# Self-attention's gate moved from the projected rows to the columns of its weight, and the order of every engine laid out anew

## What is computed

```python
attn_out = attn_out.transpose(0, 2, 1, 3).reshape(B, N, H)
attn_out = attn_out @ W_proj + b_proj
x = x + gate_a[:, None] * attn_out
q_c = _ln(x) @ W_qc + b_qc
```

## Time and profile before

| what | value |
|---|---|
| three runs, median (lowest to highest) | 2955.99 us (2954.45 to 2956.05) |
| the profiled execution, its own time | 2951.26 us |
| its span | 2949.5 us |
| mean granted clock of TensorE | 0.972 |
| PE busy | 2782.5 us, 94% |
| PE weight loads busy | 2278.2 us, 77% |
| VectorE busy | 1760.4 us, 60% |
| ScalarE busy | 1535.3 us, 52% |
| GpSimd busy | 700.2 us, 24% |

### The profile page before, as it was taken

The page is one execution under the profiler, slowest core; times in us unless marked ns, Lnnn a source line. Parts: engine busy times, 40 slices in busy tenths (PEclk is TensorE's granted clock), DMA queues, the critical chain, the costliest instruction groups (busy, mean ns, idle before and its releaser), DMA issues. The chain is left out here.

```text
span 2949.5 us, 61879 instructions
## 1 busy us (share of the span) xinstructions
PE 2782.5 (94%) x23508; PEld 2278.2 (77%) x23508; DVE 1760.4 (60%) x3583; ACT 1535.3 (52%) x2701; POOL 700.2 (24%) x760
## 2 busy tenths in 40 slices
PE   5999999994899999999999999999999999999997
PEld 4999999993577777777777777777777777777766
DVE  1344444434567777667667677666666666666642
ACT  2444444431356555555555565565565556555653
POOL 3344443331112222222222122122122121121211
PEclk7999999996699999999999999999999999999998
DMA  5222221003343443544554434544445435435421
GB/s 168 72 81 79 68 68 39 25 9 105 72 100 96 112 108 93 120 101 109 120 118 106 113 97 106 108 104 105 122 102 141 101 89 114 97 91 110 99 64 34
DMA packets 276951, 277.90 MB, mean 94 GB/s; under 512 B 90352, under 2 KB 206433, under 8 KB 276657
## 3 DMA queue, kind: packets, MB, share of 16 engines
q1 hardware_dynamic: 264752, 251.26, 35.8%
q10 hardware_dynamic: 11904, 22.68, 2.3%
HBM read 99.03 MB, written 29.56 MB: 44 GB/s over the span
## 5 line engine op out<-in xcount | busy, mean ns | idle before, releaser
L1544 ACT ACTIVATE p_f<-score 128x1024 f32<-128x1024 f32 (+1 forms) x576 | 560.6, 1019 | 340.2 <-PE obank L2165 157.9
L1821 DVE TENSOR_REDUCE m_a<-score 128x4 f32<-128x1024 f32 x384 | 457.6, 1217 | 51.9 <-PE score L2131 51.8
L2235 PE MATMUL gbank<-w,h_c 128*128 128x256 f32 x1536 | 401.4, 396 | 1.2 <-ACT h_c L1561 0.9
L2235 PEld LDWEIGHTS gbank<-w,h_c 128*128 128x128 f32 x1536 | 276.0, 192 | 48.3 <-ACT h_c L1561 1.1
L965 PE MATMUL m_ps<-m_comb,m_w 128*128 128x256 f32 x2304 | 300.5, 286 | 0.0
L965 PEld LDWEIGHTS m_ps<-m_comb,m_w 128*128 128x128 f32 x2304 | 284.8, 190 | 3.1 <-issue 1.7
L1425 POOL TENSOR_TENSOR res_a<-res_a,bias_a 128x512 f32<-128x512 f32 x48 | 64.6, 1346 | 666.9 <-DMA bias_a<-rows_L 666.9
L638 ACT ACTIVATE m_hf<-m_ps,tab 128x256 f32<-128x256 f32 x192 | 80.5, 470 | 253.3 <-PE m_ps L965 253.3
L580 POOL TENSOR_TENSOR m_hhl<-m_hf,m_hhl 128x512 fp32r<-128x512 f32 x96 | 125.2, 1304 | 328.8 <-DVE m_hhl L804 328.8
L2165 PE MATMUL obank<-p_f,v_s 128*20 128x256 f32 x3072 | 200.0, 391 | 0.0
L1433 POOL TENSOR_TENSOR c_rstd<-c_mv,eps 128x2 f32<-128x2 f32 x48 | 9.3, 194 | 774.6 <-DVE c_mv L1774 774.6
(11 more groups left out here) (234 smaller groups left out, 5561.2 us busy)
## 6 DMA issues: line engine op xcount, KB each, us to landing
k_cat<-k_hl SPq DMA_DIRECT2D x288, 128.0 KB, 3.6
q_cat<-q_hl SPq DMA_DIRECT2D x288, 128.0 KB, 4.2
qc_cat<-qc_hl SPq DMA_DIRECT2D x288, 128.0 KB, 3.2
split_L<-m_cut SPq DMA_DIRECT2D x24, 512.0 KB, 5.3
x_a<-x_after_L SPq DMA_DIRECT2D x48, 256.0 KB, 4.0
res_a<-x_after_L SPq DMA_DIRECT2D x48, 256.0 KB, 2.8
kc_cat<-kc_hl SPq DMA_DIRECT2D x288, 39.0 KB, 1.9
x_after_L<-y_c SPq DMA_DIRECT2D x32, 256.0 KB, 3.2
```

The costliest lines, as they stand in the source:

```text
L1544: e.activation(p_f[i % 4][0:n, :], score[i % 2].ap[0:n, :, :].rearrange("p h n -> p (h n)"), ACT.Exp, scale=SCALE).then_inc(ex.sem, 1)
L1821: e.tensor_reduce(m_a[:, :, i::NPAIR].rearrange("p t h -> p h t"), score[i % 2].ap[:, :, :].rearrange("p h (t k) -> p h t k", t=TT), AX.X, ...
L2235: mm = e.matmul(B_DOWN.ap[:, tt, :], h_c[:, k, tt * P:(tt + 1) * P], weights_of(d)["w2"][:, k, :], start=(k == 0), stop=(k == MC - 1))
```

## The change

Before, VectorE multiplied the projected rows by the gate and GpSimd added the residual. Now GpSimd multiplies the columns of w_o by the gate (`self_out_gated`, o_gated, one unit ahead), PE multiplies oT_a by o_gated, and VectorE adds x_b, which already holds x plus the bias, straight from the bank into x_b (`self_sum`). The tile res_a is gone: x is loaded into x_b. The loads, and the order of the calls on all five engines, are changed as well.

```diff
-                x_load(a, res_a, S["A_x"])
+                    e.wait_ge(*S["K_res"].at(a - 1))
+                    e.wait_ge(*S["K_xt"].at(a - 1))
+                x_load(a, x_b, S["A_x"])
...
-                    bias_added(res_a, res_a, bias_a[:, :], S["A_res"])
-
-            def self_sum(a):
-                if live(a):
-                    e.wait_ge(*S["T_y"].at(a))
-                    e.wait_ge(*S["A_res"].at(a))
-                    e.tensor_tensor(x_b[:, :, :], x_b[:, :, :], res_a[:, :, :], ALU.add).then_inc(S["T_xb"].sem, 1)
+                    bias_added(x_b, x_b, bias_a[:, :], S["A_res"])
+
+            def self_out_gated(a):
+
+                if not live(a):
+                    return
+                e.wait_ge(*S["A_gate"].at(a))
+                if a:
+                    e.wait_ge(*S["T_op"].at(a - 1))
+                if a % NB == 0:
+                    e.wait_ge(*W_in["o"].at(a // NB))
+                e.tensor_tensor(o_gated[:, :, :], W["o"][:, :, :], gate_a[:, :].unsqueeze(1).to_broadcast([P, CC, D]),
+                                ALU.mult).then_inc(S["T_og"].sem, 1)
...
-            def self_gated(a):
+            def self_sum(a):
                 if not live(a):
                     return
                 e.wait_ge(*S["T_op"].at(a))
-                e.wait_ge(*S["A_gate"].at(a))
-                if a:
-                    e.wait_ge(*S["K_res"].at(a - 1))
-                    e.wait_ge(*S["K_xt"].at(a - 1))
-                e.tensor_tensor(x_b[:, :, :], B_T.ap[:, :, :], gate_a[:, :].unsqueeze(1).to_broadcast([P, TT, D]),
-                                ALU.mult).then_inc(S["T_y"].sem, 1)
+                e.wait_ge(*S["A_res"].at(a))
+                e.tensor_tensor(x_b[:, :, :], B_T.ap[:, :, :], x_b[:, :, :], ALU.add).then_inc(S["T_xb"].sem, 1)
...
-                weights_in(a, "o")
-                turn(B_T, S["T_y"], a)
-                by_token(B_T, 0, oT_a, W["o"])
-                by_token(B_T, 1, oT_a, W["o"]).then_inc(S["T_op"].sem, 1)
+                e.wait_ge(*S["T_og"].at(a))
+                turn(B_T, S["T_xb"], a)
+                by_token(B_T, 0, oT_a, o_gated)
+                by_token(B_T, 1, oT_a, o_gated).then_inc(S["T_op"].sem, 1)
```

The order of GpSimd's calls, whole, since the prediction follows it:

```diff
-                context_rstd(n - 2)
+                context_rstd(a)
+                self_residual(a)
+                cross_rstd(a)
+                self_out_gated(n - 2)
+                mlp_sum(d)
+                mlp_residual(c)
+                self_rstd(n)
+                mlp_rstd(n - 4)
                 cross_residual(a)
-                self_residual(n - 2)
-                mlp_sum(n - 5)
-                self_rstd(n)
-                mlp_residual(n - 4)
-                self_sum(n - 2)
-                cross_rstd(n - 2)
-                mlp_rstd(n - 3)
```

More of the change, by code:

```diff
@@ L1134, in stats @@
             return sb(n + "_st", [P, TT, 6]), sb(n + "_mv", [P, TT, 2]), sb(n + "_rstd", [P, TT])
-        x_a, res_a = tile("x_a"), tile("res_a")
+        x_a = tile("x_a")
         xT_a, xT_b, xT_c = (sb(n, [P, 2, CC, NT], F32R) for n in ("xT_a", "xT_b", "xT_c"))
@@ L1141, in blocks @@
         bias_a, gate_a = sb("bias_a", [P, D]), sb("gate_a", [P, D])
+        o_gated = sb("o_gated", [P, CC, D])
         q_hl, k_hl = sb("q_hl", [P, 2, CC, NT], F32R), sb("k_hl", [P, 2, CC, NT], F32R)
@@ new lines, in _ @@
+                self_weights(n - 2, 7)
+                cross_max_high(n - 3)
+                next_queries_keys(q)
+                self_heads(n - 2, 0)
+                next_cross_queries(a)
+                next_rest(n)
+                next_up_high(c)
+                self_heads(n - 2, 1)
+                next_self_out(n - 2)
+                next_cross_out(b)
+                mlp_modulated(n - 4)
+                cross_weights(n - 3, 0)
+                cross_weights(n - 3, 1)
+                cross_weights(n - 3, 2)
@@ new lines, in _ @@
+                cross_weights(n - 3, 3)
+                cross_heads(n - 3, 0)
+                gelu_table(n - 4)
+                cross_heads(n - 3, 1)
+                next_values(n - 1)
+                mlp_act(n - 4, 0)
+                mlp_act(n - 4, 1)
+                mlp_act(n - 4, 2)
+                context_out(n - 2)
+                self_modulated(n)
+                self_max_high(n - 1)
+                cross_keys_high(n - 2)
+                next_up_low(n - 4)
+                cross_x_out(n - 2)
@@ L1762, in _ @@
+                keys_high(n)
+                mlp_act(n - 4, 3)
+                cross_queries_high(n - 2)
+                queries_high(n)
+                exp_table(n - 4)
+                self_weights(n - 1, 0)
+                self_weights(n - 1, 1)
+                self_weights(n - 1, 2)
+                self_weights(n - 1, 3)
+                self_weights(n - 1, 4)
+                self_weights(n - 1, 5)
         @block.vector
@@ L2404, in _ @@
                 self_plain(m, 2)
-                down(d, 6)
-                down(d, 7)
+                self_plain(m, 3)
+                mlp_turned(c)
+                values(m, 0)
                 cross_scores(b, 0)
-                self_plain(m, 3)
-                values(m, 0)
-                mlp_turned(c)
+                values(m, 1)
                 cross_scores(b, 1)
                 cross_scores(b, 2)
-                values(m, 1)
                 cross_values(b, 0)
+                up(c, 0)
@@ L2424, in _ @@
                 self_projected(a)
                 context_turned(a)
-                self_plain(m, 6)
-                self_plain(m, 7)
-                up(c, 2)
+                self_turned(q)
+                self_max_rows(m)
+                cross_keys_values(a)
+                keys(q)
+                cross_turned(a)
+                up(c, 3)
+                cross_queries(a)
+                cross_recips_spread(b)
+                queries(q)
+                self_scores(n - 2, 0)
+                self_scores(n - 2, 1)
@@ new lines, in _ @@
+                cross_projected(b)
+                down(n - 5, 0)
+                down(n - 5, 1)
+                down(n - 5, 2)
+                down(n - 5, 3)
+                down(n - 5, 4)
+                self_scores(n - 2, 2)
+                self_scores(n - 2, 3)
+                cross_plain(n - 3, 0, 0)
+                cross_plain(n - 3, 0, 1)
+                self_values(n - 2, 0)
+                cross_plain(n - 3, 1, 0)
+                self_scores(n - 2, 4)
+                cross_plain(n - 3, 1, 1)
@@ new lines, in _ @@
+                self_scores(n - 2, 5)
+                cross_plain(n - 3, 2, 0)
+                cross_plain(n - 3, 2, 1)
+                self_values(n - 2, 1)
+                cross_plain(n - 3, 3, 0)
+                self_scores(n - 2, 6)
+                self_scores(n - 2, 7)
+                cross_plain(n - 3, 3, 1)
+                down(n - 5, 5)
+                cross_max_rows(n - 3)
+                down(n - 5, 6)
+                self_plain(n - 1, 0)
+                self_plain(n - 1, 1)
```

183 lines of the change are left out of this document (55 added, 128 removed).

## The result

| | before | after |
|---|---|---|
| median, device us | 2955.3 (2954.45 to 2956.05, 4 runs) | 3037.3 (3032.17 to 3041.35, 4 runs) |
| profiled execution, us (span) | 2951.3 (2949.5) | 3034.8 (3033.0) |
| mean granted clock of TensorE | 0.972 | 0.956 |

The ratio is 1.0277, 95% interval 1.0259 to 1.0295. The change makes the kernel slower, as forecast, but by 82 us instead of 47, and the time lies 2 us above the range.

What follows compares the result with a forecast made beforehand. PE, busy 94% of the span, was taken as the bound. To the profiled 2951.3 us, -13 - 55 + 85 + 30 = +47 gave 2998 us, or 3003 us for the median; range 2908 to 3035.

Steps and rivals of the forecast that it cites:

- Part 1: PE's matmuls: changes of the array's use fall from 29 to 26 a turn, -0.27 us a turn, -13 us in 48.
- part 3: PE's old wait at xn_b's transpose, for ScalarE's modulation of x_a, goes: -1.15 us a turn, -55 us in 48.
- the second rival, VectorE ahead: No GpSimd operation in VectorE's way; new waits 0.6 us in L1 and L2, 0.2 in L3: 2911 us; chance 25%.
- Part 4: L1 and L2, after the projection: GpSimd parts xn_b's scalings; PE waits 2.65 us a turn (lower bound 0.6), +85 us.
- Part 5: L3: x_a's cast and rest wait for GpSimd; PE waits 1.85 us (0.2 if unhindered), +30 us in 16 units.
- Part 6: Elsewhere in the turn: zero, 24 us to either side; filling and draining: zero, 5 us to either side.
- the third rival, "waits cool the array": Waits of 2 us a turn pull PE's mean clock to 0.97: 64 us more, about 3065 us; 8% with Late rows.
- Late rows: An SP row transfer misses PE by 1 us every turn: 48 us more, about 3050 us; 8% with the clock.
- The first rival: L1 and L2: y_c stays out between xn_b's halves, PE waits 1.4 us: +45 instead of +85, 2963 us; chance 17%.
- Part 2: VectorE's and GpSimd's replaced operations keep their size, engine sums hardly move, and SP costs nothing: zero.

Runs made afterwards that it cites:

- e1: Changed kernel with GpSimd's o_gated, y_c and res_c moved behind the next x_a's statistics (self_rstd): 2916.1 us, ratio to before 0.988.
- e3: Changed kernel with 14 extra matmuls, results overwritten, ahead of PE's wait for xn_b in L1 and L2: 2997.9 us, ratio to before 1.016.
- e2: Changed kernel with only GpSimd's o_gated moved behind self_rstd: 2943.9 us, ratio to before 0.997.
- e6: Changed kernel with GpSimd's y_c and res_c moved behind self_rstd, o_gated left in place: 2946.1 us, ratio to before 0.998.
- e7: e1's orders with the old gate (VectorE multiplies, GpSimd adds res_a), next layer's w_o load also later: 3040.3 us, ratio to before 1.029.
- e5: Kernel before, orders kept, with the gate change alone, o_gated ahead of GpSimd's bias addition to x_b: 2952.5 us, ratio 1.000.
- e4: Kernel before, orders kept, with the gate change alone, o_gated between GpSimd's bias addition to x_b and y_c: 2973.9 us, ratio 1.007.

## Why the prediction was wrong by its size

- **Part 1, part 3** are borne out together with the lower bounds of parts 4 and 5: the second rival, VectorE ahead, was priced at 2911 us with no GpSimd operation in the way, and e1, which is that case made by hand, has 2916. Whether the array's changes are worth 13 us of that was not measured by itself; their counts, 29 and 26 a turn, are what one turn of each trace has. No run shows that leaving a 32-row product costs nothing (in before the group behind its two matmuls starts 0.42 us after them, 2014.01 to 2014.43; two whole ones take 0.24), but as both orders have two such products a turn, the difference does not hang on it.
- **Part 4** named the mechanism and its place. xn_b's pair was to take 2.5 us or more and takes 2.62; PE was to wait 1.9 us and waits 2.00; o_gated was to start within 0.1 us of t_rstd's end and does. Of the 0.25 us for unit q's split 0.1 to 0.2 shows, in the keys' row of 1.80 us (twelve such matmuls take 1.60 to 1.70 elsewhere). Of the 0.5 us for vc_s 0.35 is there: `up` starts 0.74 us after the transposes do, and 0.39 in the earlier trace rows. Turns of 46.1 us are what three turns around 1600 us have, and e3's are 46.3.
- **One thing missing in part 4**, small: the two short operations of t_rstd take turns as well. Beside VectorE's cast and subtraction they take 0.39 and 1.16 us instead of 0.20 and 0.70. I had taken t_rstd 1.05 us after the statistics, and it came 1.7 us after. It came at 3.6 by the forecast's count instead of 2.94, and xn_b's pair ended at 6.26 instead of 6.0; since PE, too, was ready 0.1 us later than counted, its wait hardly changed. (The sum for the split was off the other way: 2.35 and 0.69 make 3.04, which is where it ended, and not 3.13.) In e1 it is what is left, 0.59 us of VectorE's waiting.
- **Part 5** holds: turns of 45.4 us against 45.3. PE waits for both parts of xT_a, as said: its weight loads 8.6 us for the cast and 14.1 for the rest in 12 turns (0.7 and 1.2 us; forecast 0.65 and 1.2), its matmuls, which still have work when the loads stop, 3.2 and 11.7 (0.3 and 1.0). The turn is 1.8 us longer than e1's 43.6.
- **The agreement of the rest is partly luck.** Without the clock (e3) the turns are 46.3 and 45.45 us, not 46.1 and 45.3: 32 and 16 of them make 8 us more than the sum. The whole of e3's execution came out 2.5 us below it all the same: what its span holds beside 48 such turns is 786 us, in before 797. Part 6 had put filling and draining at zero, 5 us to either side.
- **The step that failed** is the third rival, "waits cool the array", and the way it was placed. It was an alternative at 8% together with a late row, not a term of the sum, though the forecast itself made the wait of about 2 us that it needs. Its price was for 48 units and spread evenly (64 us); measured, it is 1.5 us in 26 turns, 39 us, and as much by e3 against after. The mean clock of 0.97 that it supposed is what L2 has, and its 1.3 us a turn was near; L3 has none of it. What I held against it, that 1.15 us every turn leaves the clock up, is true but was a row about a wait half as long. A condition that my own likeliest case fulfils had to be in that case's sum, or at least in its upper bound: 2998 + 4.7 + 39 is 3042, and the range ended at 3035.
- **The first rival**, GpSimd comes in once, did not happen, since y_c was issued 0.05 us before o_gated ended. Its price held L3's 30 us, which e2 and e6 do not have: 2933 without them, against a measured 2944 and 2946.
- **Late rows** hardly happened in after: PE's matmuls wait 1.0 us in all for rows of q_cat between 900 and 2850 us (before 4.3). e7 shows the mechanism, 75 us with the clock's part in it, for a load that is held until the gate has been used.
- **Part 2's zero** for the engines holds in e5 and fails in e4: the same o_gated costs 21 us if it stands in front of an operation that VectorE waits for. As the change has it, the place was not free either.

## What to carry to other kernels

Place a long GpSimd operation by what VectorE runs at that moment, not by whether GpSimd is idle: two in a row that need nothing of each other can part a pair of VectorE's operations, and here four lines of order were worth 121 us of 3037. If the likeliest case puts a new wait of some microseconds into a busy TensorE, put the lower clock behind it into that case's sum or bound, and compare it with rows of waits as long as the new one. A gain on a chain counts only once that chain is what is waited for last, so measure each half of a change with the other left out.

## What the hardware showed that I had not expected

- A wait of 2.00 us in a turn of 46 us was followed by 3.4 us at 1.2 GHz in 26 of 29 turns; at 855, 1568 and 1660 us the same wait was not. (The turn at 1614 us had a wait of 1.35 us and no fall.) Waits of 1.05 to 1.07 us in 29 turns of e2 and 28 of e6, and of 0.98 us in before, were followed by none in L1 and L2. But the length of the wait alone does not decide: in e4 two waits for oT_a, of 0.80 us at 1393 us and 1.36 us at 1622 us, were followed by 3.4 us at the lower level. Why these fell and the three at 2.00 us were spared is open.
- Adding 14 matmuls a turn that compute nothing took 39 us off the time (e3).
- Even GpSimd operations on two numbers a partition take turns with VectorE: 0.20 us becomes 0.39 beside a cast, and 0.70 becomes 1.15 beside a subtraction.
- An operation of 128x512 on GpSimd (1.27 us) holds up a VectorE scaling that is issued 0.06 us behind it until it has ended: the pair takes 1.68 us instead of 0.73, behind y_c as behind o_gated.
